# Post-layernorm block with a ternary top-k feed-forward: the setup rebuilt, and the flag's place in PSUM

## What is computed

```python
x = layernorm(x + x @ (W + delta_W).T)                 # 512 -> 512
z = x @ ternary_quant(W_syn).T + b_syn                  # 512 -> 2048
topv, _ = top_k(z, 204); thresh = topv[:, -1:]
hidden = where(z >= thresh, relu(z), 0)
out = hidden @ ternary_quant(W_out).T + b_out           # 2048 -> 512
x = layernorm(x + layernorm(x + out, gamma, beta))
# ternary_quant(W): s = mean|W|; clip(round(W / (s + 1e-8)), -1, 1) * s
```

## Time and profile before

| | us |
|---|---|
| median of 3 runs (658.6 to 659.12) | 658.97 |
| the profiled execution | 658.22 |
| its span, from first to last instruction | 656.4 |
| busy: PE (TensorE matmul) | 581.0 |
| busy: ACT (ScalarE) | 554.5 |
| busy: DVE (VectorE) | 545.0 |
| busy: POOL (GpSimd) | 378.8 |

### The profile page before, as it was taken

One profiled execution on the slowest core, in us unless ns is written; L12 is line 12 of the kernel. 1 busy time (PEld: TensorE's weight loads), 2 busy tenths in 40 slices (PEclk: granted clock), 3 DMA queues, 4 the chain that ended last, 5 costly groups with the idle time before them and its releaser, 6 DMA issues. The chain is left out here.

```text
span 656.4 us, 8334 instructions
## 1 busy us (share of the span) xinstructions
PE 581.0 (89%) x2374; PEld 254.5 (39%) x2374; DVE 545.0 (83%) x649; ACT 554.5 (84%) x729; POOL 378.8 (58%) x712
## 2 busy tenths in 40 slices
PE   0769478999999999999999999999999999897552
...
DVE  4557787899899898999989989989989999988761
ACT  2866766899999999999999999999999999988732
...
PEclk9779797999999999999999999999999999998777
DMA  8952044254546454645455454535564444443340
GB/s 341 391 147 49 16 96 81 55 104 83 114 96 129 98 128 97 128 82 127 97 105 120 75 116 88 115 80 124 97 130 96 98 96 88 89 97 80 81 92 36
DMA packets 184481, 71.62 MB, mean 109 GB/s; under 512 B 168048, under 2 KB 176240, under 8 KB 183792
## 3 DMA queue, kind: packets, MB, share of 16 engines
...
...
## 5 line engine op out<-in xcount | busy, mean ns | idle before, releaser
L507 ACT ACTIVATE junk<-z_sb,t_col 128x2048 f16<-128x2048 f32 x128 | 254.9, 1992 | 11.9 <-POOL t_col L406 10.9
L886 PE MATMUL z_ps<-t_syn,xhT 128*128 128x512 f16 x1024 | 234.1, 383 | 6.4 <-DMA xhT<-xh 5.8
L886 PEld LDWEIGHTS z_ps<-t_syn,xhT 128*128 128x128 f16 x1024 | 100.8, 99 | 139.5 <-issue 27.4
L896 PE MATMUL o_ps<-t_out,hT 128*128 128x512 f16 x512 | 122.8, 396 | 19.0 <-DMA hT<-hh 17.0
L871 PE MATMUL u_ps<-weff,xT_sb 128*128 128x512 f32 x256 | 120.1, 614 | 21.6 <-DVE weff L639 16.7
L387 POOL TENSOR_SCALAR tmp<-signs,dev 128x1 f32<-128x1 f32 x64 | 47.3, 739 | 140.2 <-ACT junk L507 140.1
L902 PE MATMUL o_ps<-t_out,hT 128*128 128x512 f16 x512 | 120.1, 389 | 0.0
L779 DVE SCALAR_TENSOR_TENSOR z_sb<-z_sb,thr 128x2048 f32<-128x2048 f32 x32 | 75.3, 2352 | 31.2 <-DVE flag L758 18.2
L745 DVE SCALAR_TENSOR_TENSOR z_sb<-z_ps,sc,bias_z 128x1024 f32<-128x1024 f32 x64 | 81.9, 1279 | 9.5 <-PE z_ps L886 9.5
L543 ACT ACTIVATE hh<-z_sb 128x2048 f16<-128x2048 f32 x32 | 61.1, 1911 | 30.7 <-DVE z_sb L779 30.7
L718 DVE SCALAR_TENSOR_TENSOR w_sb<-z_sb,t_col 128x2048 f32<-128x2048 f32 x32 | 75.2, 2352 | 13.2 <-POOL t_col L406 13.2
...
## 6 DMA issues: line engine op xcount, KB each, us to landing
...
z_sb<-in_w_synT SPq DMA_DIRECT2D x4, 1024.0 KB, 13.1
...
```

Of the source, the lines that this page charges most:

```text
L507: a_.activation(junk[:, n % 2, :], z_sb[:, t % ZS, :], ACT.Sign, bias=at, scale=-1.0, accum_out=signs[:, j, r:r + 1]).then_inc(counted, 1)
L886: last = mm(z_ps[:, c, b * BANK:(b + 1) * BANK], xhT[:, j, h * KD + k, :], t_syn[:, k, n0:n0 + BANK], start=k == 0 and h == 0, stop=k == K ...
L896: mm(o_ps[t % OS][:, :], hT[:, j, 0, c, :], t_out[:, c, :], start=c == 0, stop=False)
```

## The change

Setup:
- wT and dwT come in two halves of 512 KB each with a semaphore per half; `first_weights(h)` works on one half and fuses the addition with the row sum. b_syn's small load goes ahead of the W_syn chunks. The broadcast of b_syn, x of pair 1, the output weights and the vectors are issued after the first transpose; `load_out(3)` and the vectors after the second.
- The sum over |W_syn| is shared: DVE sums chunks 0, 1 and half of 3, ACT chunk 2 and the other half.
- z keeps its own scale: `bias_z` isn't multiplied, and the power of two `sc[:, 6:7]` is applied in `hi_h` (as ACT's scale operand) and in `lo_h` (tensor_tensor becomes scalar_tensor_tensor).
- TensorE runs 30 filling matmuls before `mm1(0)`, and 8 after `mm1(0)`, after `mm1(1)` and after the first `total`. `mm1(0)` waits for `weff` part by part, `mm2(0, c)` for `t_syn` chunk by chunk.
- The orders of DVE, ACT and POOL in the setup differ, as below.

Flags and order: the flag of tiles 0 to 2 lies in `o_ps[t]`, of tiles 28 to 31 in `u_ps`, of the others as before. For s = 2, 3, 4 and for s = 30, 31, `mm2(s, 1)` stands right behind `mm2(s, 0)`. For s > 32 POOL's `add_beta` stands ahead of `mean_r`, and at s = 32 ACT's `count(31, 4)` ahead of `square2`. SPREAD goes from 1.295 to 1.2945.

```diff
...
+EARLY, BETWEEN = 30, 8
...
+            if s == 1:
+                order = [0, 1, 4, 2, 3]
...
+        def flag_at(t):
+            if t < OS:
+                return o_ps[t][0:1, 0:1]
+            return u_ps[0:1, 0:1] if t >= TILES - TAIL else z_ps[0:1, 1, 0:1]
...
+            for h in range(2):
+                sp.dma_start(weff[:, 2 * h:2 * h + 2, :], wT_v[:, 2 * h:2 * h + 2, :]).then_inc(weff_loaded[h], 16)
+                sp.dma_start(dw_in[:, 2 * h:2 * h + 2, :], dwT_v[:, 2 * h:2 * h + 2, :]).then_inc(weff_loaded[h], 16)
...
+            sp.dma_start(b_in[:, :], b_syn.rearrange("(p a) -> p a", p=P)).then_inc(b_loaded, 16)
...
+            sp.dma_start(bias_z[:, :], b_syn.rearrange("(a n) -> a n", a=1).broadcast_to([P, N]))\
+                .then_inc(bsyn_loaded, 16)
+            load(1)
+            load_out(0)
+            load_out(1)
+            load_out(2)
+            transpose_x(1)
+            load_out(3)
+            for k, src in enumerate((b_out, gamma, beta)):
+                sp.dma_start(vecs[:, k, :], src.rearrange("(a n) -> a n", a=1).broadcast_to([P, D])).then_inc(vec_loaded, 16)
...
-            for s in range(LAST + 2):
+            for s in range(1, LAST + 2):
...
+            scales(-2)
...
-            scales(-2)
...
+                if s > TILES and live(l):
+                    add_beta(l)
...
-                if live(l):
+                if s <= TILES and live(l):
...
-                a_.activation(hh[:, t % 2, 0, :], z_sb[:, t % ZS, :], ACT.Copy).then_inc(h_hi, 1)
+                a_.activation(hh[:, t % 2, 0, :], z_sb[:, t % ZS, :], ACT.Copy, scale=sc[:, 6:7]).then_inc(h_hi, 1)
...
+            ln1_out(-3, 0)
+            hi_x(0)
+            sum_syn(2, 0, N)
+            sum_syn(3, 1, HALF)
+            square1(-2, 1)
...
-            ln1_out(-3, 0)
-            hi_x(0)
-            for i in range(2, 6):
-                sign_syn(i)
-            square1(-2, 1)
-            sign_syn(6)
-            sum_nnz()
+            sign_syn(2)
...
-            sign_syn(7)
+            sign_syn(3)
+            sign_syn(4)
+            sum_nnz()
+            for i in range(5, 8):
+                sign_syn(i)
...
+            square1(-1, 2)
...
-            square1(-1, 2)
-            sum_out(2)
...
+                if s == TILES:
+                    count(s - 1, 4)
...
-                if live(s - 1):
+                if live(s - 1) and 1 < s < TILES:
...
+                if s == 1:
+                    count(0, 4)
+                if live(s):
...
-            def first_weights():
...
+            def first_weights(h):
+                ks = range(2 * h, 2 * h + 2)
+                dve.wait_ge(weff_loaded[h], 32)
+                for k in ks:
+                    v.scalar_tensor_tensor(weff[:, k, :], weff[:, k, :], 1.0, dw_in[:, k, :], ALU.mult, ALU.add,
+                                           accum_out=wsum[:, k:k + 1]).then_inc(setup_step, 1)
+                nstep[0] += 2
+                dve.wait_ge(setup_step, nstep[0])
...
+                nstep[0] += 2
+                link(v.tensor_scalar(wmean[:, 2 * h:2 * h + 2], wsum[:, 2 * h:2 * h + 2], 1.0, -U_SCALE / D, ALU.add, ALU.mult))
+                for k in ks:
+                    v.tensor_scalar(weff[:, k, :], weff[:, k, :], U_SCALE, wmean[:, k:k + 1], ALU.mult, ALU.add)\
+                        .then_inc(weff_made, 1)
+            def sum_syn(k, n0, i):
+                dve.wait_ge(syn_loaded[k], 16)
+                src = syn_in[k][:, n0:N]
+                link(v.scalar_tensor_tensor(w_sb[:, n0:N], src, -1.0, src, ALU.mult, ALU.max, accum_out=psyn[:, i:i + 1]))
...
-                dve.wait_ge(abs_summed, KD)
+            def syn_scale():
...
-                v.tensor_tensor(hh[:, j, 1, :], z_sb[:, t % ZS, :], hh[:, j, 0, :], ALU.subtract).then_inc(h_lo, 1)
+                v.scalar_tensor_tensor(hh[:, j, 1, :], z_sb[:, t % ZS, :], sc[:, 6:7], hh[:, j, 0, :], ALU.mult,
+                                       ALU.subtract).then_inc(h_lo, 1)
...
+                if t == 0:
+                    dve.wait_ge(bsyn_loaded, 16)
...
-                v.tensor_copy(flag[:, :], z_ps[0:1, 1, 0:1]).then_inc(flag_read, 1)
+                v.tensor_copy(flag[:, :], flag_at(t)).then_inc(flag_read, 1)
...
-            first_weights()
+            first_weights(0)
+            first_weights(1)
...
+            sum_syn(0, 0, 0)
+            lo_x(0)
+            sum_syn(1, 0, 1)
+            sum_syn(3, HALF, KD)
+            syn_scale()
...
-            lo_x(0)
-            for i in range(3, 8):
+            spread()
+            syn_weights(3)
+            lo_x(1)
+            for i in range(4, 7):
...
+            spread_out()
+            evac(0, 0)
+            syn_weights(7)
+            evac(0, 1)
...
-            lo_x(1)
-            spread()
-            evac(0, 0)
-            evac(0, 1)
+            sum_out(2)
+            evac(1, 0)
...
-            scale_vecs()
-            evac(1, 0)
...
+            evac(1, 1)
...
-            evac(1, 1)
-            out_weights(1)
-            evac(2, 0)
...
+            out_weights(1)
...
+            evac(2, 0)
...
+            scale_vecs()
+            evac(2, 1)
...
-            evac(2, 1)
...
+                if s == 3:
+                    evac(s, 0)
...
-                if live(s):
+                if live(s) and s > 3:
...
+                    if t == 0:
+                        pe.wait_ge(weff_made, k + 1)
...
-                if c == 1:
-                    wait(pe, flag_read, t - L_SEL + 1)
+                if c == 1 and OS <= t - L_SEL < TILES - TAIL:
+                    pe.wait_ge(flag_read, t - L_SEL + 1)
...
+                    if t == 0:
+                        pe.wait_ge(t_syn_made, c * KD + k + 1)
...
+                if t < OS:
+                    pe.wait_ge(flag_read, t + 1)
...
-            def flags(s, t):
+            def flags(t):
...
-                pe.wait_ge(z_evac, 2 * upto(s - 1))
...
-                mm(z_ps[0:1, 1, 0:1], ones[:, 0:1], ok[:, t % 2:t % 2 + 1], start=True, stop=True).then_inc(flag_ready, 1)
+                if t >= TILES - TAIL:
+                    pe.wait_ge(x1_ready, TILES)
+                elif t >= OS:
+                    pe.wait_ge(z_evac, 2 * upto(t + 1))
+                mm(flag_at(t), ones[:, 0:1], ok[:, t % 2:t % 2 + 1], start=True, stop=True).then_inc(flag_ready, 1)
...
+            def keep_busy(n):
+                for _ in range(n):
+                    mm(z_ps[:, 1, BANK:BANK + P], ones[:, :], ones[:, :], start=True, stop=True)
...
-            pe.wait_ge(weff_made, KD)
+            keep_busy(EARLY)
...
+            keep_busy(BETWEEN)
+            mm1(1)
+            keep_busy(BETWEEN)
...
-            mm1(1)
-            pe.wait_ge(t_syn_made, KD)
+            keep_busy(BETWEEN)
...
-            pe.wait_ge(t_syn_made, 2 * KD)
...
+            mm2(1, 1)
...
-            mm2(1, 1)
...
+                if live(s) and not OS <= f < TILES - TAIL:
+                    mm2(s, 1)
...
-                    flags(s, f)
+                    flags(f)
...
-                if live(s):
+                if live(s) and OS <= f < TILES - TAIL:
...
```

More of the change, by code:

```diff
@@ L33 @@
 ROUNDS = 5
-SPREAD = 1.295
+SPREAD = 1.2945
 MIDDLE = TOPK - 4.5
@@ L48 @@
 ZS, XS, OS = 6, 8, 3
+TAIL = 4
 def live(t):
@@ L124, in postln_kernel @@
         flag = sb("flag", [1, 1], I32)
-        psyn = sb("psyn", [P, KD])
+        psyn = sb("psyn", [P, KD + 1])
         nsyn = sb("nsyn", [P, 1])
@@ L151, in postln_kernel @@
         x_loaded = [sem(f"x_loaded{j}") for j in range(2)]
-        weff_loaded = sem("weff_loaded")
+        weff_loaded = [sem(f"weff_loaded{h}") for h in range(2)]
         syn_loaded = [sem(f"syn_loaded{k}") for k in range(KD)]
@@ L239, in load, with load_out @@
                 sp.dma_start(xT_sb[:, j, :, :], xT_v[:, :, pair * 2 * P:(pair + 1) * 2 * P]).then_inc(x_loaded[j], 16)
-            sp.dma_start(weff[:, :, :], wT.rearrange("(k p) n -> p k n", p=P)).then_inc(weff_loaded, 16)
-            sp.dma_start(dw_in, dwT.rearrange("(k p) n -> p k n", p=P)).then_inc(weff_loaded, 16)
+            def load_out(k):
+                dst = out_in[k].rearrange("p (c d) -> p c d", d=D)
+                sp.dma_start(dst, outw_v[:, QB * k:QB * (k + 1), :]).then_inc(out_loaded[k], 16)
+            wT_v, dwT_v = (a.rearrange("(k p) n -> p k n", p=P) for a in (wT, dwT))
+            for h in range(2):
+                sp.dma_start(weff[:, 2 * h:2 * h + 2, :], wT_v[:, 2 * h:2 * h + 2, :]).then_inc(weff_loaded[h], 16)
+                sp.dma_start(dw_in[:, 2 * h:2 * h + 2, :], dwT_v[:, 2 * h:2 * h + 2, :]).then_inc(weff_loaded[h], 16)
             load(0)
+            sp.dma_start(b_in[:, :], b_syn.rearrange("(p a) -> p a", p=P)).then_inc(b_loaded, 16)
             for k in range(KD):
                 sp.dma_start(syn_in[k], syn_v[:, k, :]).then_inc(syn_loaded[k], 16)
-            sp.dma_start(b_in[:, :], b_syn.rearrange("(p a) -> p a", p=P)).then_inc(b_loaded, 16)
```

(16 more changed lines are left out.)

40 lines of the change are left out of this document (14 added, 26 removed).

## The result

The changed kernel takes **649.83 us** (median of 4 runs, 649.38 to 651.34) against 659.0 for the kernel before: a ratio of 0.9866, 95% interval 0.9849 to 0.9883. Forecast were 650.1 us and faster. The profiled execution took 649.86, 2.0 more than its span of 647.9.

A forecast was written before the change was run, and what follows sets the result against it. TensorE's pace of 17.45 us a tile bounds the middle, a second cycle close behind. Span 656.4 - 8.7 (start) - 0.2 (end) = 647.5 us; as median 658.97 - 8.9 = 650.1 us, range 645.5 to 656.0.

The forecast's parts named there:

- Weights in halves, mm1(0): Setup: weight halves done on DVE at 9.0 and 11.9 against 16.55; mm1(0) at full clock ends at 15.0, before 22.6.
- The price of filling: TensorE in the setup: each filling matmul costs 0.25 us, between 0.21 and 0.43; the 30 end at 11.4.
- Rival (a): Setup: filling matmuls cost more; total 652.6 us at 0.32 us each, 656.7 at 0.43; chance 0.22.
- The sum, chunk by chunk, tile 0: Start: sum at 23.4 against 22.75, mm2(0,0) over at 32.5 instead of 43.5, tile 0's last evacuation 10.6 us earlier.
- the third of the prediction's signs of being wrong: Start: the prediction is wrong if output loads hold xhT(0) or xhT(1).
- The walk to the middle: From tile 0's z to flag 3: below(0) 13.8 us earlier, last output weights 7.5, below(1) 8.0, below(2) 8.9.
- The fall of the clock at flag 3: TensorE waits some 3.2 us for flag 3 and its clock falls, costing 1.6 to 2.8 us; 8.7 us lead remains.
- Rival (b): TensorE keeps full clock at flag 3, or the walk to below(1) is shorter: 10.5 to 12.5 us, 647.5; chance 0.20.
- Unscaled z: Second cycle: lo_h 2.35 instead of 2.29 us, hi_h 0.08 more; nothing in the middle, 0.5 us over the last four tiles.
- rival (c): Middle: new lo_h or hi_h lengthens the second cycle in 26 tiles; 664 us at 0.9 us a tile; chance 0.05.
- The tail: Last tiles: +0.45 for order, +0.5 for scaling, -0.35 at flag 31, -0.78 from add_beta: -0.2 us, from -1.2 to +1.5.

The follow-up runs named there:

- fill60: Changed kernel with 60 instead of 30 filling matmuls before mm1(0): 655.35 us, ratio 0.9928.
- early_loads: Changed kernel with the broadcast of b_syn, x of pair 1, output weights and vectors issued ahead of the first transpose again: 662.53 us, ratio 1.0053.
- warm3: Changed kernel plus 13 filling matmuls in TensorE's queue ahead of flag 3: 646.88 us, ratio 0.9819.
- tail0: Changed kernel with flags of tiles 28 to 31 in z_ps and mm2(s,1) behind the flag for s = 30, 31 again: 649.98 us, ratio 0.9868.
- warm_tail: Changed kernel plus 26 filling matmuls ahead of each of mm3_hi(29), (30) and (31): 651.27 us, ratio 0.9884.
- again: The changed kernel run once more, no edit: 650.35 us, ratio 0.985.
- head0: Changed kernel with flags 0 to 2 in z_ps and mm2(s,1) behind the flag for s = 2 to 4 again: 649.56 us, ratio 0.9855.

## Why the prediction was right

The time was right, to 0.3 us, and so was the mechanism at the start and in the middle: the start gives all, the middle nothing. The tail, put at +0.2, gave 1.75 back. The lead at flag 4 was 1.55 us larger than forecast and the tail 1.95 worse, so the closeness of the total is in good part luck.

- **Weights in halves, mm1(0).** Forecast 9.0 and 11.9, measured 8.33 and 12.58; the second half landed late (1.42 us wait at 9.74). mm1(0) ended at 14.97, forecast 15.0.
- **The price of filling.** Taken 0.25 us a matmul between 0.21 and 0.43; measured 0.223 at full clock. They ended at 11.4, forecast 11.4, and that is luck: at 0.112 a pass the 60 are 6.7 us, so the slow passes cost 2.7 us more (an estimate: about 5 us at half rate), where 1.7 (3.4 us at half rate) were taken from `mm1(0)`. The same 60 passes took 8.35 to 9.91 us in the other profiles. The upper bound of 0.43 was no bound: a load alone takes 0.19 us, longer than a pass, so two loads and two passes without overlap would be 0.6. The estimate of 0.32 from the Trainium skill (TensorE: Matmul & The Clock Gate, Back-to-back issue gap) is not borne out: load and matmul overlap here (both are busy for all of the stretch from 2.10 to 11.40). Rival (a) falls by that, but its mechanism holds: fill60 delayed the sum by 6.7 us and the middle by 6.75.
- **The sum, chunk by chunk, tile 0.** Sum 23.4 forecast, 23.26 measured; mm2(0,0) over at 32.5 and 32.24; evac(0,1) at 40.2 and 39.80. That "`xhT(0)` is issued with one weight chunk ahead of it instead of four output chunks" is the step that carries the gain: early_loads undid it and lost 12.2 us. Output loads held neither xhT(0) nor xhT(1) (issued at 31.82, mm2(1,0) follows mm2(0,1) without a gap), the third of the prediction's signs of being wrong.
- **The walk to the middle.** below(0) 59.6 and 59.44, last output weights 85.9 and 85.45, below(1) 87.3 and 86.73, below(2) 103.9 and **102.70**, flag 3 127.7 and 126.78. The steps were forecast 0.2 to 1.2 us too late, flag 3 by 0.9.
- **The fall of the clock at flag 3** (the term mis-sized). Forecast 3.2 us idle and 1.6 to 2.8 us lost, with 0.5 more; measured 2.77 idle and 1.61 lost (19.08 against 17.47), and warm3 took 1.58 of it back. The lead at flag 4 is 10.25 where I took 8.7: 0.9 from the walk, 0.6 from this term. Rival (b) named a lead of 10.5 to 12.5 for a shorter walk or no fall; the walk was the shorter one it had in mind, and the lead came out just below its range.
- **Unscaled z.** 0.06 on DVE as forecast and 0.093 on ACT against 0.08; flags stay 17.47 apart, so rival (c) falls. That rests on durations and the unchanged period; the step was not undone on its own.
- **The tail: the step that failed.** Forecast up to flag 31 a loss of 0.6 (0.45 + 0.5 - 0.35), measured 0.44: the order cost 0.23 where 0.45 was taken, some 0.3 is left for unscaled z, which I put at 0.5, and the gain of 0.35 at flag 31 came to 0.07, since `ok` was held by `add_beta` once the count was out of the way. After flag 31 I counted only the 0.78 us of `add_beta`, and it did come out. Not in the sum were mm3_hi(31) starting 5.61 instead of 4.44 us after its transpose is issued, and then taking 0.67 longer at the lower clock. Instead of gaining 0.2 the tail gave back 1.75. Tail0 says that the order of the last tiles has 0.23 of it; 1.31 lie behind flag 31.

Also not undone on their own: the weights in halves, the shared sum over |W_syn|, the early load of b_syn, and SPREAD. Their share of the start is argued from the rows, not shown.

What the late start of mm3_hi(31) hangs on is open. In thirteen of the fourteen profiles it begins within 0.14 us, either side, of the end of the issue of the second transpose (624.64 + 3.10 and 627.86 above; 634.22 + 2.19 and 636.33 before); only in warm_tail, where filling stood ahead of it, 0.4 later. That issue takes 3.1 us in again, head0, tail0, early_loads and the changed kernel, and 2.0 to 2.2 in the other nine; no edit among them changes these transposes. What makes it long was not found, and nothing was tried against it.
